# Second attention's stack turns in two of the score banks, root steps set apart, stages placed anew

## The reference

```
x = x + attn_a(layernorm(x))    # linear attention, 16 heads of 16: phi = elu + 1, causal running sums
x = x + ffn(layernorm(x))       # relu(x W1q + b1) W2q + b2, 1024 hidden, W1q and W2q in {-1, 0, 1}
x = x + attn_b(layernorm(x))    # 16 query heads on 4 key heads, RMS norm of q and k, rotary, window 64, softmax
x = x + ffn(layernorm(x))       # the same weights as above
```

## Time and profile before

| | us |
|---|---|
| median of three runs | 3016.64 |
| profiled execution | 3018.86 |
| its span, first to last instruction | 3017.0 |

### The profile page before, as it was taken

How to read it: one execution, slowest core, us unless ns; L and a number is a source line. 1 busy time by engine, 2 the same in 40 slices (tenths; PEclk the granted TensorE clock), 3 DMA queues, 4 the chain that set the end, 5 groups by cost and what they waited for, 6 DMA issues and landing times.

```text
span 3017.0 us, 75500 instructions
## 1 busy us (share of the span) xinstructions
PE 2801.0 (93%) x25924; PEld 2277.3 (75%) x25924; DVE 2297.0 (76%) x5983; ACT 1746.8 (58%) x3589; POOL 500.9 (17%) x1047
## 2 busy tenths in 40 slices
PE   5789999999999999999999999999999999999976
PEld 4677778877777877777777777777777777777765
DVE  6577787777788777788777788777788777788753
ACT  2356565566655566665566655566656556656553
POOL 4111111111111111111111111101111111111110
PEclk8899999999999999999999999999999999999997
DMA  2000000000000000000000000000000000000000
GB/s 69 8 11 17 17 17 3 14 17 17 17 17 4 13 17 17 17 17 13 4 17 17 17 17 17 3 14 17 17 17 17 3 14 17 17 17 17 4 11 15
DMA packets 42050, 45.04 MB, mean 15 GB/s; under 512 B 2640, under 2 KB 41360, under 8 KB 42000
## 3 DMA queue, kind: packets, MB, share of 16 engines
q1 hardware_dynamic: 42000, 44.40, 4.8%
HBM read 21.32 MB, written 16.78 MB: 13 GB/s over the span
## 4 chain that ended last, share of the span: by engine, by line
PE 68%; DVE 16%; issue 7%; ACT 4%; DMA 3%; DVEq 1%; POOL 0%; SPq 0%; ACTq 0%; POOLq 0%
PE Q L380 18%; PE Y L464 12%; PE HID L440 11%; PE Q L594 4%; PE Q L621 3%; PE HID L388 3%; PE Q L857 3%; DVE a_s L1440 2%; PE Q L644 2%; DMA out<-x 2%; DVE x L1348 2%; ACT a_qz L1170 2%; PE Q L757 2%; PE Q L794 1%; PE Q L873 1%
## 5 line engine op out<-in xcount | busy, mean ns | idle before, releaser
L989 ACT ACTIVATE f_r<-HID,b1c 128x512 f32<-128x512 f32 x512 | 355.1, 694 | 386.0 <-PE HID L440 333.7
L464 PE MATMUL Y<-w2t,f_hh 128*128 128x256 f32 x2048 | 539.4, 296 | 8.5 <-DVE f_hl L1334 8.5
L464 PE MATMUL Y<-w2t,f_hl 128*128 128x256 f32 x2048 | 512.4, 283 | 0.0
L440 PE MATMUL HID<-ff_xh,w1t 128*128 128x512 f32 x1024 | 440.1, 430 | 22.2 <-ACT f_hh L990 16.1
L1334 DVE TENSOR_TENSOR f_hl<-f_r,f_hh 128x512 fp32r<-128x512 f32 x512 | 351.2, 686 | 85.2 <-ACT f_hh L990 80.6
L440 PE MATMUL HID<-ff_xl,w1t 128*128 128x512 f32 x1024 | 410.9, 401 | 0.0
L464 PEld LDWEIGHTS Y<-w2t,f_hh 128*128 128x128 f32 x2048 | 390.1, 190 | 22.0 <-DVE f_hl L1334 14.5
L464 PEld LDWEIGHTS Y<-w2t,f_hl 128*128 128x128 f32 x2048 | 391.1, 191 | 7.4
L990 ACT ACTIVATE f_hh<-HID,b1c 128x512 fp32r<-128x512 f32 x512 | 354.4, 692 | 0.0
L440 PEld LDWEIGHTS HID<-ff_xh,w1t 128*128 128x128 f32 x1024 | 195.9, 191 | 100.8 <-issue 31.7
L1440 DVE TENSOR_TENSOR a_s<-Q,cst 128x512 f32<-128x512 f32 x384 | 246.2, 682 | 27.8 <-PE Q L594 27.7
(11 more groups left out here) (197 smaller groups left out, 7519.1 us busy)
## 6 DMA issues: line engine op xcount, KB each, us to landing
x<-in_x SPq DMA_DIRECT2D x32, 512.0 KB, 4.2
out<-x SPq DMA_DIRECT2D x32, 512.0 KB, 3.1
b_vm<-b_v SPq DMA_DIRECT2D x64, 96.0 KB, 2.1
x<-in_w SPq DMA_DIRECT2D x2, 512.0 KB, 4.3
a_s<-in_w_qkv SPq DMA_DIRECT2D x1, 768.0 KB, 5.0
cst<-in_const SPq DMA_DIRECT2D x1, 645.0 KB, 6.1
ff_xn<-in_w SPq DMA_DIRECT2D x1, 512.0 KB, 7.0
f_r<-in_w SPq DMA_DIRECT2D x1, 512.0 KB, 6.7
```

What stands on the lines that cost most here:

```text
L440: mm = pe.matmul(banks[fb % 2][:], w1t[:, k, fb * P:(fb + 1) * P], src[:, k, :], start=(k == 0 and j == 0), stop=(k == KB - 1 and j == 1))
L464: mm = pe.matmul(Y[t // 2][:, (t % 2) * D:(t % 2 + 1) * D], h[:, fb % 2, t * P:(t + 1) * P], w2t[:, fb, :], start=False, stop=(fb == FB - ...
L989: act.activation(f_r[:, fb % 2, :], banks[fb % 2][:], ACT.Relu, bias=b1c[:, fb:fb + 1]).then_inc(f_rr, 1)
```

## The change

Three things change. The turns of tiles 1 to 3 go into Q[0] (q) and Q[1] (k), two of the score banks: `turn_q(t)` now waits for two of the four exponents of the tile before, `turn_k(t)` for three, and `turn_numer(t)` waits for the residual of the tile before. Function `roots(group)` becomes `root_step(group, n)`, the same ten instructions, one per call, and the calls stand between other calls of VectorE's list. And calls of all three lists of TensorE, ScalarE and VectorE are placed anew, in both halves. No instruction is added or left out; GpSimd's and SyncE's lists stay as they are.

```diff
--- before.py
+++ after.py
@@ -247,7 +247,7 @@
         def turn_bank(t, j):
-            return Q[3] if j and t == 0 else Q[2]
+            return (Q[0], Q[1])[j] if t else (Q[2], Q[3])[j]
         QK_ORDER = (2, 3, 0, 1)
         def table(name, t, lo, hi):
@@ -664,26 +664,26 @@
                 qkv(s.b, t, NSEQ)
         return
     up(5)
+    down(4)
+    qk(a, 2)
     values(0)
-    qk(a, 2)
     up(6)
-    down(4)
     qk(a, 3)
     down(5)
     up(7)
+    turn_keys(0)
     values(1)
-    turn_keys(0)
     own_norm()
     turn_keys(1)
     down(6)
     state(0)
     scores(0)
-    up(0)
     state(1)
     down(7)
+    up(0)
     numer(0, 0)
+    state(2)
     numer(0, 1)
-    state(2)
     up(1)
     turn_numer(0)
     bias()
@@ -718,8 +718,8 @@
     qkv(s.b, 1, a + 1)
     project(3)
     qkv(s.b, 2, a + 1)
+    down(3)
     qkv(s.b, 3, a + 1)
-    down(3)
 def phase2(s):
     b, n, own, carry = s.b, second_turn(s.b), first_turn(s.a), second_turn(s.c)
@@ -747,12 +747,9 @@
         if t == 0:
             pe.wait_ge(a_out, a_done * NT)
-        elif t == 1:
-            pe.wait_ge(b_te, b * 8 + 1)
         else:
-            pe.wait_ge(b_out, b * NT + t - 1)
+            pe.wait_ge(b_ex, (b * NT + t - 1) * KVH + 2)
         for r in range(REP):
             mm = pe.transpose(turn_bank(t, 0)[:, r * P:(r + 1) * P].bitcast(F32R),
                               b_qs[:, t % 2, KVH * r:KVH * (r + 1)].rearrange("p h s d -> p (h s d)"), ident_r[:])
@@ -761,7 +758,7 @@
     def turn_k(t):
         if t:
-            pe.wait_ge(b_te, b * 8 + 2 * t + 1)
+            pe.wait_ge(b_ex, (b * NT + t - 1) * KVH + 3)
         for m in range(2):
             mm = pe.transpose(turn_bank(t, 1)[:, m * P:(m + 1) * P].bitcast(F32R),
                               b_ks[:, t % 2, m].rearrange("p h s d -> p (h s d)"), ident_r[:])
@@ -862,10 +859,7 @@
     def turn_numer(t):
         pe.wait_ge(b_ne, b * NT + t + 1)
-        if t < NT - 1:
-            pe.wait_ge(b_te, b * 8 + 2 * t + 4)
-        else:
+        if t:
             pe.wait_ge(b_out, b * NT + t)
         for i in range(2):
@@ -896,43 +890,43 @@
     up(6)
     turn_q(0)
     turn_k(0)
+    down(5)
     scores(0)
     up(7)
-    down(5)
+    down(6)
     numer(0)
+    own_norm(0)
     turn_q(1)
-    own_norm(0)
-    turn_k(1)
-    down(6)
     turn_numer(0)
     down(7)
+    turn_k(1)
     own_norm(1)
     turn_y(0)
     scores(1)
     bias()
     up(0)
+    turn_q(2)
     project(0)
+    turn_k(2)
     numer(1)
-    turn_q(2)
     up(1)
-    turn_k(2)
-    down(0)
     turn_numer(1)
     scores(2)
+    down(0)
     turn_y(1)
     up(2)
     project(1)
     turn_q(3)
+    turn_k(3)
     numer(2)
+    down(1)
     next_norm(0)
-    turn_k(3)
-    down(1)
     scores(3)
+    turn_numer(2)
     next_norm(1)
     down(2)
-    turn_numer(2)
+    turn_y(2)
     numer(3)
-    turn_y(2)
     qk(s.next_a, 0, b)
     project(2)
     up(3)
@@ -1093,13 +1087,13 @@
     qk_exp(0)
     qk_exp(1)
     relu(5)
+    qk_exp(2)
     values(0)
-    qk_exp(2)
     relu(6)
     qk_exp(3)
     relu(7)
+    keys(0)
     values(1)
-    keys(0)
     own_norm()
     keys(1)
     relu(0)
@@ -1112,8 +1106,8 @@
     next_norm(0)
     evacuate_numer(2)
     next_norm(1)
+    relu(3)
     y_hi(2)
-    relu(3)
     evacuate_numer(3)
     relu(4)
     y_hi(3)
@@ -1189,36 +1183,36 @@
         return
     if s.a is not None:
         raw(b, 2)
+    if s.a is not None:
+        raw(b, 3)
     relu(5)
     stack_hi(0)
-    if s.a is not None:
-        raw(b, 3)
+    relu(6)
     evacuate_q(0)
     evacuate_k(0)
-    relu(6)
     exps(0)
+    relu(7)
     stack_hi(1)
-    relu(7)
     evacuate_numer(0)
+    own_norm(0)
+    stack_hi(2)
     evacuate_q(1)
-    own_norm(0)
     evacuate_k(1)
-    stack_hi(2)
     own_norm(1)
     y_hi(0)
     exps(1)
     relu(0)
     evacuate_q(2)
+    evacuate_k(2)
     evacuate_numer(1)
-    evacuate_k(2)
     stack_hi(3)
     relu(1)
     y_hi(1)
     exps(2)
     relu(2)
     evacuate_q(3)
+    evacuate_k(3)
     evacuate_numer(2)
-    evacuate_k(3)
     next_norm(0)
     exps(3)
     next_norm(1)
@@ -1493,27 +1487,27 @@
     low(5)
     phi(1)
     phi(2)
+    own_apply()
     low(6)
+    phi(3)
     by_parity(0)
-    phi(3)
-    own_apply()
+    low(7)
     by_parity(1)
-    low(7)
     own_norm_lo()
     state(0)
     mask(0)
     state(1)
     finish_first(s)
-    low(0)
     state(2)
     next_stats()
+    low(0)
     normalise(0)
     mask(1, (0, 1))
     y_lo(0)
     mask(1, (2, 3))
     residual(0)
+    next_apply()
     low(1)
-    next_apply()
     normalise(1)
     mask(2, (0, 1))
     y_lo(1)
@@ -1521,19 +1515,19 @@
     next_norm_lo(0)
     residual(1)
     low(2)
-    f1_stats(0)
     next_norm_lo(1)
     normalise(2)
     mask(3, (0, 1))
     mask(3, (2, 3))
     y_lo(2)
+    f1_stats(0)
+    f1_stats(1)
+    residual(2)
     low(3)
-    residual(2)
-    f1_stats(1)
+    normalise(3)
+    low(4)
+    y_lo(3)
     f1_stats(2)
-    normalise(3)
-    y_lo(3)
-    low(4)
     residual(3)
     f1_stats(3)
@@ -1570,38 +1564,40 @@
         dve.tensor_reduce(b_ss[:, t, :], b_sq[:, t % 2].rearrange("p (h j) -> p h j", j=HD), X,
                           ALU.add).then_inc(b_ss_s, 1)
-    def roots(group):
+    def root_step(group, n):
         tiles = (slice(0, 1), slice(1, NT))[group]
-        n = (1, NT - 1)[group]
         step = b * 18 + 9 * group
...
+        if n == 0:
+            dve.wait_ge(b_ss_s, b * NT + (1, NT)[group])
+            dve.tensor_scalar(var, b_ss[:, tiles], 1.0 / HD, RMS_EPS, ALU.mult, ALU.add).then_inc(b_ch, 1)
+            return
+        dve.wait_ge(b_ch, step + n)
+        if n == 1:
...
     def cosines(t):
         j = b * NT + t
@@ -1678,28 +1674,46 @@
         return
     sums(0)
     cosines(0)
-    roots(0)
+    root_step(0, 0)
+    root_step(0, 1)
+    sums(1)
+    root_step(0, 2)
+    root_step(0, 3)
+    root_step(0, 4)
     rotate(0)
+    root_step(0, 5)
+    root_step(0, 6)
+    root_step(0, 7)
+    root_step(0, 8)
+    root_step(0, 9)
+    norm_qk(0)
+    sums(2)
+    low(5)
+    stack_lo(0)
+    sums(3)
+    root_step(1, 0)
+    root_step(1, 1)
+    root_step(1, 2)
+    root_step(1, 3)
+    low(6)
+    root_step(1, 4)
     cosines(1)
-    norm_qk(0)
-    sums(1)
-    rotate(1)
-    stack_lo(0)
-    sums(2)
     if guarded:
         maxima(0)
-    sums(3)
-    low(5)
+    root_step(1, 5)
+    rotate(1)
+    root_step(1, 6)
+    root_step(1, 7)
+    root_step(1, 8)
     if guarded:
         maxima(1)
-    roots(1)
+    cosines(2)
+    root_step(1, 9)
+    rotate(2)
     norm_qk(1)
-    cosines(2)
-    low(6)
+    own_apply()
     stack_lo(1)
-    own_apply()
     low(7)
-    rotate(2)
     norm_qk(2)
     own_norm_lo(0)
     normalise(0)
@@ -1708,42 +1722,42 @@
         maxima(2)
         maxima(3)
     own_norm_lo(1)
+    stack_lo(2)
     y_lo(0)
     cosines(3)
     rotate(3)
-    stack_lo(2)
+    norm_qk(3)
     residual(0)
-    norm_qk(3)
     low(0)
     next_stats()
     if guarded:
         maxima(4)
         maxima(5)
     normalise(1)
+    y_lo(1)
     stack_lo(3)
-    y_lo(1)
     low(1)
-    residual(1)
     next_apply()
+    if guarded:
+        maxima(6)
     low(2)
     if guarded:
-        maxima(6)
-    f2_stats(0)
+        maxima(7)
+    residual(1)
     next_norm_lo(0)
-    if guarded:
-        maxima(7)
-    f2_stats(1)
     normalise(2)
     next_norm_lo(1)
+    f2_stats(0)
     y_lo(2)
     residual(2)
     normalise(3)
+    f2_stats(1)
     low(3)
     y_lo(3)
+    low(4)
     residual(3)
     f2_stats(2)
     f2_stats(3)
-    low(4)
 dve.wait_ge(x_in, 16)
 norm_stats(at, 0, x0, range(NT))
```

More of the change, by code:

```diff
@@ new lines, in root_step @@
+                        if n == 0:
[4 more added lines that the diff above has]
+                        if n == 1:
+                            dve.tensor_scalar(root.bitcast(mybir.dt.int32), var.bitcast(mybir.dt.int32),
+                                              -0.5, float(ROOT_GUESS), ALU.mult, ALU.add).then_inc(b_ch, 1)
+                        elif n == 2:
+                            dve.tensor_tensor(t, root, root, ALU.mult).then_inc(b_ch, 1)
+                        elif n == 3:
+                            dve.tensor_tensor(t, t, var, ALU.mult).then_inc(b_ch, 1)
+                        elif n == 4:
+                            dve.scalar_tensor_tensor(out=t, in0=t, scalar=-10.0 / 3.0, in1=t, op0=ALU.add, op1=ALU.mult).then_inc(b_ch, 1)
+                        elif n == 5:
+                            dve.scalar_tensor_tensor(out=root, in0=t, scalar=5.0, in1=root, op0=ALU.add, op1=ALU.mult).then_inc(b_ch, 1)
+                        elif n == 6:
+                            dve.scalar_tensor_tensor(out=t, in0=root, scalar=-0.5 * ROOT_SCALE ** 2, in1=root,
+                                                     op0=ALU.mult, op1=ALU.mult).then_inc(b_ch, 1)
+                        elif n == 7:
+                            dve.tensor_tensor(t, t, var, ALU.mult).then_inc(b_ch, 1)
```

(7 more changed lines are left out.)

25 lines of the change are left out of this document (removed).

## The result

The changed kernel took 2944.85 us (median of four runs, 2938.50 to 2952.70) against 3015.31 for the kernel before in four: a ratio of 0.9767, 95% interval 0.9753 to 0.9782, so 70.5 us less. The prediction was 2946. Its total is right; the sum behind it is not. What made that up stood in the sum at nothing or at less: the falls of the clock vanished from the full rounds, and the end of the run, where the pipeline drains, gave 16 us.

What follows compares the result with a forecast made beforehand. TensorE was taken to be bound by standing in order behind short VectorE-ScalarE-TensorE chains. Second half 2.0 plus first half 0.3 gave 2.3 us a round, times 31 rounds 71 us: 2946 us, own range 2930 to 2965, overall 2918 to 2995.

Steps and rivals of the forecast that it cites:

- 0.96 us won: Second half, tile 0: down(5) fills the 0.79 us wait of scores(0), leaving one down chunk more done at numer(0), 0.96 us.
- raw(3) ahead of relu(5) at nothing: Second half, ScalarE: raw(3), about 0.9 us, moved ahead of relu(5) costs nothing, since ScalarE waits for up(5) there anyway.
- turn_q(1) 0.8 later, scores(1) 1.2 us earlier: Second half, tile 1: turn_q(1) at 1696.15 instead of 1695.36, yet scores(1) at 1698.75 instead of 1699.93.
- 1.1 here: Store, load and tile 2: finish_second, the next x and normalise(1) come about 1.1 us earlier, whatever else was won.
- Turns waiting for exponents at 0: Tiles 2 and 3: the added waits of turn_q and turn_k for exponents of the tile before cost 0.
- qk(0) 2.0 earlier: End of second half, tile 3: qk(0) at 1717.2 instead of 1719.19, 2.0 us earlier, carried into the next half.
- First half: First-attention half: reordered calls win 0.3 us a round, mainly low(0) behind state(2) releasing turn_numer(0) sooner.
- 1, a fall in every round: Second half behind numer(0): thin work lowers the clock in all 31 rounds, 1.13 us each; 2970 us, chance 0.14.
- 2, the gain ends at the load: normalise(1) comes 1.1 us earlier, but the 0.9 behind it and the first half's gain are lost; 2985 us, chance 0.16.
- 3's first half: Rival of more gain: clock falls vanish (11 us), and besides 3.2 us a round are won; 2909 us, chance 0.06.
- 4: Whole round: the same waits return under other names, less than 0.3 us a round; 3010 to 3025 us, chance 0.05.
- 5: Ahead of scores(1): nine alternating ScalarE-VectorE hops each take 0.3 us more, making the kernel slower; 3031 us, chance 0.07.

Runs made afterwards that it cites:

- e6_sines: The changed kernel with GpSimd's sines of tile 2 moved behind the root of the feed-forward norm; 2946.42 us, ratio 0.9774 to the kernel before.
- e2_down5: The changed kernel with down(5) back behind up(7) in TensorE's list, nothing else; 2966.90 us, ratio 0.9826 to the kernel before.
- e3_roots: The changed kernel with each group's ten root steps in one piece, tile 0's ahead of the sums of tile 1; 3028.01 us, ratio 1.0035 to before.
- e7_early: The changed kernel with VectorE's sums and cosines of second-half tile 0 moved into the end of the first half; 2924.56 us, ratio 0.9704 to before.
- e10_load: e8_qkv3 with the load of the next x ahead of the store of out on SyncE; 2919.73 us, ratio 0.9673 to before.
- e1_banks: The kernel before with only the two score banks for the turns of tiles 1 to 3 and their waits; 2983.65 us, ratio 0.9889.
- e9_down5: The kernel before with only down(5) ahead of scores(0) on TensorE and low(5) ahead of the sums of tile 2 on VectorE; 3016.08 us, ratio 0.9998.
- e8_qkv3: e7_early with qkv(3) behind up(5) on TensorE and relu(5) ahead of raw(3) on ScalarE; 2920.26 us, ratio 0.9697 to before.
- e4_phase1: The kernel before with the changed kernel's first-half lists on TensorE, ScalarE and VectorE, second half as before; 3074.99 us, ratio 1.0183.
- e5_whole: The changed kernel with each group's root steps in one piece, the sums of tile 1 ahead of the first group; 2978.13 us, ratio 0.9883 to before.
- e12_tile2: e8_qkv3 with VectorE's cosines and rotation of tile 2 behind low(7), and ScalarE's stack_hi(1) ahead of relu(7); 2940.73 us, ratio 0.9750 to before.
- e11_split: e10_load with two of own_apply's four tiles moved behind stack_lo(1) on VectorE; 2927.27 us, ratio 0.9705 to before.

## Why the prediction was right, and where its sum was not

Offsets are from the start of qkv(2), before and after.

- **Tile 0, "0.96 us won".** Half right. scores(0) no longer waits, but it came 0.30 later, not at the same time, because turn_q(0) came 0.15 later where 0.2 earlier was forecast (+7.27 to +7.42): norm_qk(0) was quick, as hoped (0.49), but two root steps beside GpSimd's sines took 0.37 and 0.42. The Trainium skill's page "SBUF — State Buffer" (SBUF: two separate sides) says that a VectorE instruction with two SBUF inputs and a GpSimd instruction that reads SBUF hold a shared port pair in turn, each for its whole length; the trace agrees, the two steps took 0.18 and 0.21 in e6_sines, where the sines ran beside another step, and that one took 0.42. And e2_down5 shows that this fill was worth nothing by itself in a round.
- **raw(3) ahead of relu(5) at nothing.** Right: up(5) stands at +3.06 in both, up(6) waits 0.42 against 0.41. e3_roots shows on what that hangs: the sums of tile 1 early among the root steps. The forecast had these at 0.1 to 0.2 us of the steps alone.
- **Tile 1, "turn_q(1) 0.8 later, scores(1) 1.2 us earlier".** This is the term that was mis-sized. turn_q(1) came 1.39 later (+13.62 to +15.01), since own_apply began at 1743.21, behind an unbroken VectorE list, and stack_lo(1) behind it; scores(1) came 0.51 earlier. The trace of before already held the number. VectorE was without a gap there too, and its list reached stack_lo(1) at 1694.60; the new list puts own_apply (1.3) and rotate(2) (0.4) ahead of that and takes nothing away. The forecast has own_apply end at 1695.45, so begin at 1694.15, 0.45 earlier than the old list got there, and its sum has no term for rotate(2). With 1.7 more and 0.3 saved among the other steps, 1.4 later is what was measured. The half's busy share (VectorE 30.89 of 42.11 us), from which room in VectorE was read, hides such a stretch. e7_early points the same way: a start 0.88 us earlier on VectorE gave 0.47 a round.
- **Store, load, tile 2, "1.1 here".** finish_second 0.61 earlier, normalise(1) 0.74: the shortfall of tile 1 handed on. The load was no bound of its own (e10_load).
- **Turns waiting for exponents at 0; turn_q(3)'s 0.61 gone; qk(0) 2.0 earlier.** The first two right (in after one such wait in the whole run, 1.3 us in the drain; e1_banks for the second). qk(0) came 1.46 earlier: from normalise(1) on 0.72 of the forecast's 0.9 came. First half 0.07 instead of 0.3.
- **Falls left as they were, and a sum of 31 equal rounds.** Wrong both, and both gave more than forecast. Falls were worth some 9 us, up to 12 with the first interval. The drain gave 16.4 where 3 x 2.3 = 6.9 stood in the sum for its three intervals; e2_down5 with the new second half ends alike (219.1), e9_down5 with the old one like before (232.4).

Against the forecast, the profiled pair gave 0.65 x 27 = 17.5 us less in the rounds, some 10 more through falls and the first interval, 9.5 more in the drain and 7.2 in the part up to the first store, for which the count of 31 intervals has nothing: 9 more in all. Its spans differ by 10 more than the medians, and on these the total met. So it met by luck: errors of both signs cancelled. (Three of the rivals' totals, 2985, 2909 and 3031, are reckoned from the profiled 3018.9, the forecast from 3016.6; the 2 us change nothing.)

**The rivals.** 1, a fall in every round: none in 28. Behind numer(0) the new order has only transposes and two waits of 0.32 and 0.60, and the clock stayed at 2.4 GHz; the falls of before stood behind three waits, of which the last was 0.80. The rule of the Trainium skill's "TensorE: Matmul & The Clock Gate" (Part 4: PE-mode transpose) that a transpose does not count as busy in the same way spoke for this rival; no run here separates transposes from the waits beside them. 2, the gain ends at the load: in size nearest of the rivals (1.1 a round), and nothing came of the first half (0.07), as it said; its cause fell, since of the 0.9 behind normalise(1) 0.72 came, and in e10_load, on the lists of e8_qkv3, an earlier load gave nothing. 3's first half, falls vanish, came true, its 3.2 a round did not. 4 and 5 fell; 5 had looked at the right place, ahead of scores(1), but not ScalarE and VectorE in turns set it: VectorE's list alone was without a gap.

What stays open: what sets off a fall in some rounds and not in others that have the same waits (e9_down5 moved falls and halved them, it did not end them). The four kernels with the third wait of 0.79 us (before, e1_banks, e2_down5, e4_phase1) held 8 to 13 falls in their 28 full rounds; seven without it held none; three without it still held some, 3 in e5_whole, 6 in e9_down5 and 20 in e3_roots, each with another wait of 0.9 to 1.8 us in the half's first 15 us, though e12_tile2 has one of 0.99 and held none. Open is also how much of the drain's 16 us is clock and how much shorter chains.

## What to carry to other kernels

Idle time of TensorE between short chains can cost twice: by itself, and by the clock. Here the third of three waits that stand close together, 0.79 us, was worth nothing in a quiet round, but with it in place 13 of 28 rounds held a fall and without it none (e2_down5 against the changed kernel, some 20 us over the run). It has to be filled without a new wait behind it (e9_down5). Before a wait is costed, look for the engine that is without a gap from the start of the stage to the release, and add up all calls that an edit puts ahead of the release in its list. In such a stretch taking work out ahead helped (e7_early), while the reorderings tried inside it moved the wait (e11_split, e12_tile2). Count rounds, falls and the fill and drain of a pipeline as separate terms.
